# Three matrix projections of a gated linear-attention layer: from three fp32r products each to one plain fp32 product

## The chip, the cores and the metric

The kernel runs on one core of one Trainium2 chip. The metric is the device time of one launch in microseconds (us). The kernel before takes 194.22 us in the median of 3 runs (193.96 to 195.49).

## The reference, cut to what matters

The input `x` is 4 batches of 512 tokens with 256 features. It is layer-normed, projected to q, k, v and a low-rank gate, run through a chunked linear attention with 16 heads of 16 features, gated and normed by head, projected out, and multiplied by a small FFN branch that is rounded to fp8.

```python
xn = _layernorm(x, axis=-1)
q = silu(einsum('bnd,de->bne', xn, Wq).reshape(b, n, H, hd))    # k, v alike with Wk, Wv
o, _ = lightning_attn(q, k, v, log_decay)
gate = einsum('bnk,kd->bnd', einsum('bnd,dk->bnk', xn, Wg1), Wg2)
o = group_rmsnorm_fused_gate(o, gate, norm_w, H)
s = einsum('bnd,de->bne', o, Wo)
g = silu(ffn(xn, input2, scale, scale1))                        # both operands rounded to fp8
out = x + s * g
```

## The kernel before, in words

The work is cut into 16 chunks of 128 tokens, four to a batch. Each engine runs a prologue and then 18 steps, `step(i, j)`; the steps are software-pipelined by hand, so that one step holds different stages of neighbouring chunks. The order on each engine is the order in which its `step` function calls its helpers, and semaphores join the engines. For chunk n (`num(i, j)`) the step of TensorE (PE) does: the score products of n (`scores`, L1082, four groups r = 0 to 3), the gate product (L1068), the state update (L1108), the output projection of chunk n-2 (`project_o`, L1177), the K/V projection of chunk n+1 (`project_kv`), the Q/gate projection of chunk n+1 (`project_qg`), transposes for chunks n+1 and n+2 (L1009, L1021, L1063 and others), the products of masked scores with v (`from_chunk`, L1121), the FFN product (L1046), the products with the state (L1140), the transpose of the normed output (L1169), and the addition of the parts by products with the identity (`add_chunk`, L1150, L1153, L1157). Each score group goes through VectorE (DVE), which multiplies it with the decay mask (`mask`, L717). `from_chunk` waits for all four.

Three projections are computed to about fp32 accuracy from three fp32r products. Each operand is split in a high part, the value rounded to fp32r, and a low part, the rest: hi*hi + hi*lo + lo*hi, for each of two halves of the 256 contracted features. So each projection is 6 matmul calls: L1029, L1031 and L1034 for K/V (512 columns) and Q/gate (272 columns), and L1177 for the output projection (256 columns).

- ScalarE (ACT) makes the high part of the transposed x out of PSUM (`high_xT`, L484) and of the transposed output (`high_oT`, L537). DVE makes the low parts (`low_xT`, L703, `low_oT`, L783), after ACT.
- The weights are split once in the prologue: ACT makes the high parts of Wk and Wv (L576), DVE those of Wq and Wg1 (L854) and the low parts (`low_w`, L805). Wo, scaled by the norm weights (L828), is split in the first step (L628, L832).
- In the DVE prologue `low_w` and `low_xT` stand ahead of the layer-norm statistics of chunk 1 (L663), and `low_g1` (L707), which needs the Q/gate projection of chunk 0, comes some instructions later.

All other matmuls, but the gate product in fp32r and the FFN in bf16, are already plain fp32: `scores`, `state_step`, `from_chunk`, `from_state`, `add_chunk`. `keep_warm` (L1184) issues plain fp32 matmuls of 128 columns with no use but to keep PE busy: 11, 3 and 3 calls in the prologue and 6 in the tail.

Of the kernel before, what the change touches and what calls it, by code (L numbers as in the profile page):

```python
# [13 lines left out]
P = 128  # L14
# [3 lines left out]
def layer_kernel(nc, x, log_decay, Wq, Wk, Wv, Wo, Wg1, Wg2, norm_w, W2, scale, scale1, out):  # L18
# [34 lines left out]
    with ExitStack() as ctx:  # L53
# [9 lines left out]
        w_hi = sb("w_hi", [P, KH, NW], F32R)  # L63
        w_lo = sb("w_lo", [P, KH, NW], F32R)
        wo_f32 = sb("wo_f32", [P, KH, D])
        wo_scaled = sb("wo_scaled", [P, KH, D])
        wo_hi = sb("wo_hi", [P, KH, D], F32R)
        wo_lo = sb("wo_lo", [P, KH, D], F32R)
# [52 lines left out]
        xT_hi = sb("xT_hi", [P, KH, P], F32R)  # L121
        xT_lo = sb("xT_lo", [P, KH, P], F32R)
# [25 lines left out]
        oT_hi = sb("oT_hi", [P, KH, P], F32R)  # L148
        oT_lo = sb("oT_lo", [P, KH, P], F32R)
# [39 lines left out]
        s_whi = sem("w_hi_ready")  # L189
        s_wlo = sem("w_lo_ready")  # L190
# [20 lines left out]
        s_xThi = sem("xT_hi_ready")  # L211
        s_xTlo = sem("xT_lo_ready")
# [32 lines left out]
        s_oThi = sem("oT_hi_ready")  # L245
        s_oTlo = sem("oT_lo_ready")
# [230 lines left out]
        def _(act):  # L477
            a = nc.scalar

            def high_xT(i, j):  # L480
                act.wait_ge(s_xTps, num(i, j) + 1)

                need(act, s_qgps, num(i, j))
                a.activation(xT_hi[:], ps_xT, ACT.Copy).then_inc(s_xThi, 1)  # L484
# [88 lines left out]
            def high_w(a0, b0):  # L573

                for kk in range(KH):
                    a.activation(w_hi[:, kk, a0:b0], w_f32[:, kk, a0:b0], ACT.Copy).then_inc(s_whi, 1)  # L576

            def prologue(act):

                act.wait_ge(s_pool, 1)  # L580
                a.activation(table_load[:], eps_col[:], ACT.Exp)
                act.wait_ge(s_w, 32)
                high_w(0, Q0)
                normalise(0, 0)
                act.wait_ge(s_dvec, 3)
                a.activation(lag_decay[:], lag_logdecay[:], ACT.Exp).then_inc(s_actc, 1)
                high_xT(0, 0)
# [12 lines left out]
                copy_kT(0, 0)  # L600
                copy_qT(0, 0)
                copy_g1T(0, 0)
                high_xT(0, 1)
                act.wait_ge(s_pool, 15)
                part_v(0, 0)
                scale_y(0, 1)

            def step(act, i, j):
# [16 lines left out]
                if first:  # L625

                    act.wait_ge(s_woready, 2)
                    a.activation(wo_hi[:], wo_scaled[:], ACT.Copy).then_inc(s_woready, 1)  # L628
                if nxt:
                    copy_xqT(i, j + 1)  # L630
                if norm:
                    high_xT(i, j + 2)
# [9 lines left out]
                if known(i, j - 1):  # L642
                    high_oT(i, j - 1)
# [9 lines left out]
        def _(dve):  # L653
# [147 lines left out]

            def low_w(a0, b0, first):
                for kk in range(KH):
                    dve.wait_ge(s_whi, first + kk + 1)
                    v.tensor_tensor(w_lo[:, kk, a0:b0], w_f32[:, kk, a0:b0], w_hi[:, kk, a0:b0].bitcast(F32), ALU.subtract).then_inc(s_wlo, 1)  # L805
# [24 lines left out]
            def low_wo():  # L830
                dve.wait_ge(s_woready, 3)
                v.tensor_tensor(wo_lo[:], wo_scaled[:], wo_hi[:].bitcast(F32), ALU.subtract).then_inc(s_woready, 1)  # L832

            def prologue(dve):
# [54 lines left out]
                low_xT(0, 1)  # L889
# [3 lines left out]
            def step(dve, i, j):  # L893
# [8 lines left out]
                if not cur:  # L902
# [7 lines left out]
                    if back:  # L910
                        newton(8, RS_STEPS)
                        head_norm_last(i, j - 1)
                        low_oT(i, j - 1)
                    else:
                        add_x_last(i, j - 2)
                    return
                if not nxt:
# [11 lines left out]
                    low_oT(i, j - 1)  # L929
# [48 lines left out]
                if norm:  # L978
                    low_xT(i, j + 2)
                if first:  # L980
                    low_wo()
# [11 lines left out]
                if back:  # L993
                    low_oT(i, j - 1)
# [5 lines left out]
        def _(pe):  # L1000
# [23 lines left out]
            def project(i, j, dst, a, b, s_done, s_free, free):  # L1024

                pe.wait_ge(s_xThi, num(i, j) + 1)
                need(pe, s_free, free)
                for kk in range(KH):
                    t.matmul(dst, xT_hi[:, kk], w_hi[:, kk, a:b], start=(kk == 0), stop=False)  # L1029
                for kk in range(KH):  # L1030
                    t.matmul(dst, xT_hi[:, kk], w_lo[:, kk, a:b], start=False, stop=False)  # L1031
                pe.wait_ge(s_xTlo, num(i, j) + 1)
                for kk in range(KH):
                    mm = t.matmul(dst, xT_lo[:, kk], w_hi[:, kk, a:b], start=False, stop=(kk == KH - 1))  # L1034
# [137 lines left out]
            def project_o(i, j):  # L1172
                pe.wait_ge(s_oTlo, num(i, j) + 1)
                parts = [(oT_hi, wo_hi), (oT_hi, wo_lo), (oT_lo, wo_hi)]
                for n, (lhs, rhs) in enumerate(parts):
                    for kk in range(KH):
                        mm = t.matmul(ps_out, lhs[:, kk], rhs[:, kk], start=(n == 0 and kk == 0), stop=(n == 2 and kk == KH - 1))  # L1177
                mm.then_inc(s_outps, 1)
# [7 lines left out]
            def prologue(pe):  # L1186
# [4 lines left out]
                pe.wait_ge(s_wlo, 2)  # L1191
                project_kv(0, 0)
                pe.wait_ge(s_wlo, 4)
# [8 lines left out]
            def step(pe, i, j):  # L1202
# [86 lines left out]
```

## Time and profile before

| | us |
|---|---|
| median of 3 runs | 194.22 (193.96 to 195.49) |
| span of the profiled execution | 191.7 |
| PE busy | 171.6 |
| DVE busy | 158.9 |
| POOL (GpSimd) busy | 106.3 |
| ACT busy | 103.2 |

The profile lays out one execution. Busy times are sums over an engine's instructions. The chain of waits follows the work that ended last back from the end, at each step to what released it. L12 is line 12 of the kernel. The end of a matmul in the trace is modelled and overlaps the next one's start; the distance from start to start shows what a matmul costs in a row of them.

### The profile page before, as it was taken

How to read it: one execution, taken by the hardware profiler on the slowest of the kernel's cores; microseconds unless marked ns; L12 is line 12 of the kernel's file. 1: busy time of each engine (PE TensorE's matmuls, PEld its weight loads, DVE VectorE, ACT ScalarE, POOL GpSimd, SP SyncE). 2: the span in 40 equal slices, each digit the busy share in tenths (PEclk: the TensorE clock that was granted, in tenths of full speed). 3: DMA queues.
4: the chain of work that ended last, by engine and by line, in shares of the span. 5: the costliest groups of instructions: out<-in, count | busy, mean ns of one | idle time of the engine just before them, and what ended most of it. 6: DMA issues, size and time to landing. Idle time of an engine off the chain costs nothing.

```text
span 191.7 us, 6387 instructions
## 1 busy us (share of the span) xinstructions
PE 171.6 (90%) x1998; PEld 129.5 (68%) x1998; DVE 158.9 (83%) x548; ACT 103.2 (54%) x283; POOL 106.3 (55%) x181
## 2 busy tenths in 40 slices
PE   4867459999999999999999999999999999998392
PEld 4755238667776777777767777777767777776181
DVE  1869995889989898989897979898979798968672
ACT  3385336293848475665656473838383838372200
POOL 6954772555656465657574756565646556551210
PEclk9979966999999999999999999999999999999967
DMA  5383300000000010000000000000000000000000
GB/s 151 88 269 113 109 2 3 3 3 0 31 2 29 1 32 0 32 1 13 14 0 27 0 27 0 27 0 27 0 27 0 27 0 27 3 29 3 27 27 27
DMA packets 7199, 5.79 MB, mean 30 GB/s; under 512 B 1744, under 2 KB 7184, under 8 KB 7184
## 3 DMA queue, kind: packets, MB, share of 16 engines
q1 hardware_dynamic: 7184, 5.60, 9.3%
q8 instruction: 8, 0.13, 0.3%
q14 instruction: 7, 0.06, 0.1%
HBM read 3.50 MB, written 2.10 MB: 29 GB/s over the span
## 4 chain that ended last, share of the span: by engine, by line
PE 56%; DVE 20%; issue 12%; POOL 3%; DMA 3%; ACT 2%; DVEq 1%; SPq 1%; POOLq 0%; ACTq 0%
PE b_score L1082 9%; PE b_score L1121 9%; PE b_xo L1177 5%; PE b_att L1108 4%; DVE probs L717 4%; PE b_att L1140 3%; PE b_gate L1046 3%; PE b_xo L1169 3%; PE b_kv L1034 2%; PE b_kv L1031 2%; PE b_kv L1029 2%; PE b_qg L1029 2%; DVE shift L681 2%; PE b_att L1157 2%; DMA ld_row<-in_L_attn_log_decay_dram 2%
## 5 line engine op out<-in xcount | busy, mean ns | idle before, releaser
L717 DVE TENSOR_TENSOR probs<-b_score,decay_mask 128x512 f32<-128x512 f32 x64 | 43.5, 682 | 0.9 <-PE b_score L1082 0.5
L1082 PE MATMUL b_score<-qT,kT 32*64 32x128 f32 x512 | 31.6, 283 | 1.6 <-DVE probs L717 1.4
L545 ACT ACTIVATE xn<-x_sb,shift,rstd 128x256 f32 (+1 forms) x15 | 9.0, 602 | 42.3 <-DVE shift L681 42.3
L1082 PEld LDWEIGHTS b_score<-qT,kT 32*64 32x64 f32 x512 | 20.1, 132 | 12.3 <-issue 7.6
L374 POOL TENSOR_TENSOR state_c<-state,own_head 128x256 f32<-128x256 f32 x28 | 20.5, 734 | 11.6 <-DVE state L734 10.5
L344 POOL TENSOR_TENSOR e_sum<-e_y,e_magic 128x256 f32<-128x256 f32 x16 | 11.6, 727 | 20.5 <-DVE e_magic L692 20.5
L1121 PE MATMUL b_score<-probs,v_parity 128*32 128x128 f32 x512 | 17.9, 283 | 1.4 <-DVE probs L717 1.2
L383 POOL TENSOR_TENSOR on<-og,og_rs 128x256 f32<-128x256 f32 x15 | 9.3, 621 | 17.2 <-DVE og_rs L777 15.4
L1121 PEld LDWEIGHTS b_score<-probs,v_parity 128*32 128x32 f32 x512 | 13.6, 113 | 4.9 <-DVE probs L717 4.5
L775 DVE SCALAR_TENSOR_TENSOR og_half<-og_y,og_var 128x16 f32<-128x16 f32 x48 | 14.8, 309 | 0.7
L391 POOL TENSOR_TENSOR y<-sg,x_sb 128x256 f32<-128x256 f32 x15 | 10.9, 730 | 5.9 <-DVE sg L788 5.9
L688 DVE TENSOR_SCALAR e_exp<-e_y 128x256 int32<-128x256 int32 x16 | 4.7, 293 | 10.6 <-ACT e_y L561 10.6
L526 ACT ACTIVATE qT<-b_qk,head_parity 128x256 f32<-128x256 f32 x32 | 13.3, 472 | 0.0
L1108 PE MATMUL b_att<-kv,kd 64*64 64x64 f32 x224 | 12.8, 234 | 0.0
L347 POOL TENSOR_TENSOR e_q<-e_sum,e_magic 128x256 bf16<-128x256 f32 x16 | 12.0, 752 | 1.3
L335 POOL TENSOR_TENSOR var_eps<-mean_var,eps_col 128x1 f32<-128x1 f32 x16 | 3.2, 201 | 17.0 <-DVE mean_var L673 17.0
L681 DVE SCALAR_TENSOR_TENSOR shift<-mean_var,rstd 128x1 f32<-128x1 f32 x16 | 10.9, 683 | 1.8 <-POOL rstd L337 0.8
L353 POOL TENSOR_TENSOR xq<-e_q,e_nan 128x256 bf16<-128x256 bf16 x16 | 10.7, 670 | 2.5 <-DVE e_nan L698 2.5
L1029 PE MATMUL b_kv<-w_hi,xT_hi 128*128 128x512 f32 x32 | 10.3, 401 | 1.8 <-ACT xT_hi L484 1.8
L1108 PEld LDWEIGHTS b_att<-kv,kd 64*64 64x64 f32 x224 | 8.9, 136 | 4.3 <-issue 2.2
L1184 PE MATMUL b_score<-ident 128*128 128x128 f32 x46 | 9.4, 384 | 2.5 <-POOL ident L402 2.5
L537 ACT ACTIVATE oT_hi<-b_xo 128x256 fp32r<-128x256 f32 x16 | 6.1, 384 | 9.4 <-PE b_xo L1169 8.4
(136 smaller groups left out, 470.9 us busy)
## 6 DMA issues: line engine op xcount, KB each, us to landing
out_dram<-y SPq DMA_DIRECT2D x16, 128.0 KB, 1.7
x_sb<-in_L_attn_x_dram SPq DMA_DIRECT2D x3, 512.0 KB, 3.4
x_sb<-in_L_attn_x_dram SPq DMA_DIRECT2D x1, 384.0 KB, 4.6
w_f<-in_L_attn_Wk_dram SPq DMA_DIRECT2D x1, 256.0 KB, 2.8
w_f<-in_L_attn_Wv_dram SPq DMA_DIRECT2D x1, 256.0 KB, 3.0
w_f<-in_L_attn_Wq_dram SPq DMA_DIRECT2D x1, 256.0 KB, 3.0
w_f<-in_L_ffn_input_dram SPq DMA_DIRECT2D x1, 256.0 KB, 4.0
wo_f<-in_L_attn_Wo_dram SPq DMA_DIRECT2D x1, 256.0 KB, 3.8
```

Of the source, the lines that this page charges most:

```text
L344: g.tensor_tensor(e4_sum[:], e4_y[:], e4_magic[:], ALU.add).then_inc(s_e4p, 1)
L347: g.tensor_tensor(e4_q[:], e4_sum[:], e4_magic[:], ALU.subtract).then_inc(s_e4p, 1)
L374: g.tensor_tensor(dst[:].rearrange("p k (b c) -> p k b c", b=2), state[:].unsqueeze(2).broadcast_to([P, KH, 2, C]), own_head[:].rearrange( ...
L391: g.tensor_tensor(y[:, j % 2, :], sg[:], xs, ALU.add).then_inc(s_y, 1)
L526: a.activation(qT[:, u, :, par, :], ps_qT, ACT.Copy, scale=head_parity[:, par:par + 1]).then_inc(s_qkT, 1)
L681: v.scalar_tensor_tensor(out=shift[:, u], in0=mean_var[:, u, 0:1], scalar=-1.0, in1=rstd[:, u], op0=ALU.mult, op1=ALU.mult).then_inc(s_shi ...
L717: v.tensor_tensor(probs[:, r].rearrange("p i (b c) -> p i b c", b=2), b_score[r % 2][:, 0:4 * C].rearrange("p (i c) -> p i c", i=4).unsque ...
L775: ins = v.scalar_tensor_tensor(out=og_half[:], in0=og_y2[:], scalar=-0.5, in1=og_var[:], op0=ALU.mult, op1=ALU.mult)
L1029: t.matmul(dst, xT_hi[:, kk], w_hi[:, kk, a:b], start=(kk == 0), stop=False)
L1082: mm = t.matmul(b_score[r % 2][c * C:c * C + C, half * 2 * C:(half + 1) * 2 * C], kT[rows, u, half, c * C:c * C + C], qT[rows, u, half, :, ...
L1108: mm = t.matmul(ps_state[b * C:b * C + C, half, :], kd[rows, u, cols], kv[rows, u, D + cols.start:D + cols.stop], start=True, stop=True)
L1121: mm = t.matmul(ps_avT[32 * r:32 * r + 32, half, :], v_parity[:, u, par * D + half * P + 32 * r:par * D + half * P + 32 * r + 32], probs[: ...
```

## The change

The K/V, Q/gate and output projections use the fp32 operands as they are, with two matmul calls each in place of six. The splits of weights and activations are gone, with their tiles and semaphores. ACT's copies of the transposed x and output out of PSUM stay and now write fp32. The gate product of low rank stays in fp32r with its split.

```diff
-            def high_xT(i, j):
+            def copy_xT(i, j):
                 act.wait_ge(s_xTps, num(i, j) + 1)
                 need(act, s_qgps, num(i, j))
-                a.activation(xT_hi[:], ps_xT, ACT.Copy).then_inc(s_xThi, 1)
+                a.activation(xT[:], ps_xT, ACT.Copy).then_inc(s_xT, 1)
...
-            def high_oT(i, j):
+            def copy_oT(i, j):
                 act.wait_ge(s_oTps, num(i, j) + 1)
                 need(act, s_outps, num(i, j))
-                a.activation(oT_hi[:], ps_oT, ACT.Copy).then_inc(s_oThi, 1)
+                a.activation(oT[:], ps_oT, ACT.Copy).then_inc(s_oT, 1)
...
-                act.wait_ge(s_w, 32)
-                high_w(0, Q0)
                 normalise(0, 0)
...
-                    act.wait_ge(s_woready, 2)
-                    a.activation(wo_hi[:], wo_scaled[:], ACT.Copy).then_inc(s_woready, 1)
...
-            def low_xT(i, j):
-                dve.wait_ge(s_xThi, num(i, j) + 1)
-                need(dve, s_qgps, num(i, j))
-                v.tensor_tensor(xT_lo[:], ps_xT, xT_hi[:].bitcast(F32), ALU.subtract).then_inc(s_xTlo, 1)
...
-            def low_oT(i, j):
-                dve.wait_ge(s_oThi, num(i, j) + 1)
-                need(dve, s_outps, num(i, j))
-                v.tensor_tensor(oT_lo[:], ps_oT, oT_hi[:].bitcast(F32), ALU.subtract).then_inc(s_oTlo, 1)
...
-                low_w(0, Q0, 0)
-                low_xT(0, 0)
-                dve.wait_ge(s_wq, 32)
-                for kk in range(KH):
-                    v.tensor_copy(w_hi[:, kk, Q0:NW], w_f32[:, kk, Q0:NW]).then_inc(s_whi, 1)
-                low_w(Q0, NW, 2)
                 stats(0, 1)
...
-                low_xT(0, 1)
                 quantise_w2()
...
-                if norm:
-                    low_xT(i, j + 2)
-                if first:
-                    low_wo()
...
-                if back:
-                    low_oT(i, j - 1)
...
             def project(i, j, dst, a, b, s_done, s_free, free):
-                pe.wait_ge(s_xThi, num(i, j) + 1)
+                pe.wait_ge(s_xT, num(i, j) + 1)
                 need(pe, s_free, free)
                 for kk in range(KH):
-                    t.matmul(dst, xT_hi[:, kk], w_hi[:, kk, a:b], start=(kk == 0), stop=False)
-                for kk in range(KH):
-                    t.matmul(dst, xT_hi[:, kk], w_lo[:, kk, a:b], start=False, stop=False)
-                pe.wait_ge(s_xTlo, num(i, j) + 1)
-                for kk in range(KH):
-                    mm = t.matmul(dst, xT_lo[:, kk], w_hi[:, kk, a:b], start=False, stop=(kk == KH - 1))
+                    mm = t.matmul(dst, xT[:, kk], w_f32[:, kk, a:b], start=(kk == 0), stop=(kk == KH - 1))
                 mm.then_inc(s_done, 1)
...
                 if known(i, j + 3):
-                    pe.wait_ge(s_xTlo, num(i, j) + 4)
+                    pe.wait_ge(s_xT, num(i, j) + 4)
...
             def project_o(i, j):
-                pe.wait_ge(s_oTlo, num(i, j) + 1)
-                parts = [(oT_hi, wo_hi), (oT_hi, wo_lo), (oT_lo, wo_hi)]
-                for n, (lhs, rhs) in enumerate(parts):
-                    for kk in range(KH):
-                        mm = t.matmul(ps_out, lhs[:, kk], rhs[:, kk], start=(n == 0 and kk == 0), stop=(n == 2 and kk == KH - 1))
+                pe.wait_ge(s_oT, num(i, j) + 1)
+                for kk in range(KH):
+                    mm = t.matmul(ps_out, oT[:, kk], wo_scaled[:, kk], start=(kk == 0), stop=(kk == KH - 1))
                 mm.then_inc(s_outps, 1)
...
-                pe.wait_ge(s_wlo, 2)
+                pe.wait_ge(s_w, 32)
                 project_kv(0, 0)
-                pe.wait_ge(s_wlo, 4)
+                pe.wait_ge(s_wq, 32)
                 project_qg(0, 0)
...
-                        pe.wait_ge(s_woready, 4)
+                        pe.wait_ge(s_woready, 2)
```

## Rows read from the trace of the kernel before

**Rows 1.** The page: busy time by engine, and the chain's shares by engine.

```profile
PE 171.6 (90%) x1998; PEld 129.5 (68%) x1998; DVE 158.9 (83%) x548; ACT 103.2 (54%) x283; POOL 106.3 (55%) x181
...
PE 56%; DVE 20%; issue 12%; POOL 3%; DMA 3%; ACT 2%; DVEq 1%; SPq 1%; POOLq 0%; ACTq 0%
```

**Rows 2.** Busy time by stretch; stretches run from one `from_chunk` (L1121) to a later one.

```profile
core 0: us, PE busy (x) PEld busy (x) DVE busy (x) ACT busy (x) POOL busy (x), PEclk, DMA share, GB/s
31.00:41.05 10.05, 9.64 (x117) 7.03 (x117) 7.72 (x27) 5.83 (x17) 4.17 (x7) 0.93 0.01 3
...
60.73:70.63 9.90, 9.90 (x128) 7.51 (x132) 8.61 (x33) 5.91 (x17) 5.46 (x9) 1.00 0.05 15
...
90.56:100.40 9.84, 9.53 (x116) 7.14 (x116) 8.83 (x34) 6.21 (x18) 6.14 (x10) 1.00 0.04 13
...
41.05:169.58 128.53, 127.51 (x1590) 95.52 (x1594) 114.18 (x420) 77.68 (x219) 77.05 (x125) 1.00 0.04 14
```

**Rows 3.** The chain of waits, 95 to 118 us: start, length, engine and line.

```profile
99.67 0.69 DVE probs L717
...
100.40 1.08 PE b_score L1121 x32
...
102.77 0.45 PE b_att L1157 x4
...
104.63 0.90 PE b_xo L1177 x6
105.53 0.45 PE b_kv L1029 x2
...
107.48 0.45 PE b_qg L1029 x2
107.93 0.25 PE b_qg L1031 x2
```

**Rows 4.** Timeline of PE, 100 to 111.3 us: start, length with drain, instruction.

```profile
105.13 0.40 PE L1177 MATMUL b_xo<-wo_hi,oT_lo 128*128 128x256 f32 x2
105.36 0.61 PE L1029 MATMUL b_kv<-w_hi,xT_hi 128*128 128x512 f32 x2
...
109.32 0.29 PE L1021 MATMUL b_gate<-ident_bf,xq 128*128 128x128 bf16 x2
109.45 0.39 PE L1009 MATMUL b_xo<-ident,xn 128*128 128x128 f32 x2
109.67 0.38 PE L1061 MATMUL b_qk<-ident,q 128*128 128x128 f32 x2
```

**Rows 5.** Groups by line and shape, DVE: busy, mean ns, idle before.

```profile
L783 DVE TENSOR_TENSOR oT_lo<-b_xo,oT_hi 128x256 fp32r<-128x256 f32 x16 | 6.7, 418 | 1.3 <-ACT oT_hi L537 1.3
L703 DVE TENSOR_TENSOR xT_lo<-b_xo,xT_hi 128x256 fp32r<-128x256 f32 x16 | 6.7, 417 | 1.7 <-ACT xT_hi L484 1.7
```

**Rows 6.** Timeline of DVE, 0 to 35 us.

```profile
10.97 0.42 DVE L703 TENSOR_TENSOR xT_lo<-b_xo,xT_hi 128x256 fp32r<-128x256 f32 x1 [1.08 <-ACT xT_hi L484]
...
12.87 0.41 DVE L663 BATCH_NORM_STATS2 bn<-x_sb 128x6 f32<-128x256 f32 x1
...
15.62 0.18 DVE L707 TENSOR_TENSOR g_stack<-b_qg,g_stack 128x32 fp32r<-128x32 f32 x1
...
28.05 1.46 DVE L717 TENSOR_TENSOR probs<-b_score,decay_mask 128x512 f32<-128x512 f32 x2
```

**Rows 7.** Busy time by stretch, start-up (columns as in rows 2).

```profile
28.00:30.00 2.00, 2.00 (x21) 1.55 (x18) 1.91 (x6) 1.30 (x4) 1.30 (x3) 0.50 0.03 8
```

**Rows 8.** Timeline of PE, 159 to 192 us: the tail.

```profile
183.49 2.66 PE L1184 MATMUL b_score<-ident 128*128 128x128 f32 x12
```

**Rows 9.** The chain of waits in the last step.

```profile
187.18 0.43 DVE oT_lo L783
...
187.66 0.99 PE b_xo L1177 x6
```

More of the change, by code:

```diff
@@ L62, in layer_kernel @@
         w_f32 = sb("w_f32", [P, KH, NW])
-        w_hi = sb("w_hi", [P, KH, NW], F32R)
-        w_lo = sb("w_lo", [P, KH, NW], F32R)
         wo_f32 = sb("wo_f32", [P, KH, D])
         wo_scaled = sb("wo_scaled", [P, KH, D])
-        wo_hi = sb("wo_hi", [P, KH, D], F32R)
-        wo_lo = sb("wo_lo", [P, KH, D], F32R)
         nw_col = sb("nw_col", [P, KH])
@@ L120, in layer_kernel @@
         xq = sb("xq", [P, 2, D], BF16)
-        xT_hi = sb("xT_hi", [P, KH, P], F32R)
-        xT_lo = sb("xT_lo", [P, KH, P], F32R)
+        xT = sb("xT", [P, KH, P])
         xqT = sb("xqT", [P, KH, P], BF16)
@@ L147, in layer_kernel @@
         on = sb("on", [P, D])
-        oT_hi = sb("oT_hi", [P, KH, P], F32R)
-        oT_lo = sb("oT_lo", [P, KH, P], F32R)
+        oT = sb("oT", [P, KH, P])
         sg = sb("sg", [P, D])
@@ L210, in layer_kernel @@
         s_xqTps = sem("xqT_in_psum")
-        s_xThi = sem("xT_hi_ready")
-        s_xTlo = sem("xT_lo_ready")
+        s_xT = sem("xT_ready")
         s_xqT = sem("xqT_ready")
@@ L244, in layer_kernel @@
         s_oTps = sem("oT_in_psum")
-        s_oThi = sem("oT_hi_ready")
-        s_oTlo = sem("oT_lo_ready")
+        s_oT = sem("oT_ready")
         s_outps = sem("out_in_psum")
@@ L571, in copy_avT @@
                 a.activation(avT[:], ps_avT, ACT.Copy).then_inc(s_av, 1)
-            def high_w(a0, b0):
-                for kk in range(KH):
-                    a.activation(w_hi[:, kk, a0:b0], w_f32[:, kk, a0:b0], ACT.Copy).then_inc(s_whi, 1)
             def prologue(act):
@@ L586, in prologue @@
                 a.activation(lag_decay[:], lag_logdecay[:], ACT.Exp).then_inc(s_actc, 1)
-                high_xT(0, 0)
+                copy_xT(0, 0)
                 act.wait_ge(s_small, 64)
@@ L602, in prologue @@
                 copy_g1T(0, 0)
-                high_xT(0, 1)
+                copy_xT(0, 1)
                 act.wait_ge(s_pool, 15)
@@ L631, in step @@
                 if norm:
-                    high_xT(i, j + 2)
+                    copy_xT(i, j + 2)
                 if nxt:
@@ L642, in step @@
                 if known(i, j - 1):
-                    high_oT(i, j - 1)
+                    copy_oT(i, j - 1)
                 if nxt:
@@ L800, in add_x_last @@
                 v.tensor_tensor(y[:, j % 2, :], sg[:], x_sb[:, num(i, j), :], ALU.add).then_inc(s_y, 1)
-            def low_w(a0, b0, first):
-                for kk in range(KH):
-                    dve.wait_ge(s_whi, first + kk + 1)
-                    v.tensor_tensor(w_lo[:, kk, a0:b0], w_f32[:, kk, a0:b0], w_hi[:, kk, a0:b0].bitcast(F32), ALU.subtract).then_inc(s_wlo, 1)
             def quantise_w2():
@@ L828, in scale_wo @@
                     v.tensor_scalar(wo_scaled[:, kk], wo_f32[:, kk], nw_col[:, kk:kk + 1], None, ALU.mult).then_inc(s_woready, 1)
-            def low_wo():
-                dve.wait_ge(s_woready, 3)
-                v.tensor_tensor(wo_lo[:], wo_scaled[:], wo_hi[:].bitcast(F32), ALU.subtract).then_inc(s_woready, 1)
             def prologue(dve):
@@ L928, in step @@
                     gate_o(i, j)
-                    low_oT(i, j - 1)
                     return
@@ L977, in step @@
                 newton(10, RS_STEPS)
-                if norm:
-                    low_xT(i, j + 2)
-                if first:
-                    low_wo()
                 if nxt:
@@ L992, in step @@
                     gate_o(i, j)
-                if back:
-                    low_oT(i, j - 1)
             steps(step, prologue)(dve)
@@ L1172, in project_o @@
             def project_o(i, j):
-                pe.wait_ge(s_oTlo, num(i, j) + 1)
-                parts = [(oT_hi, wo_hi), (oT_hi, wo_lo), (oT_lo, wo_hi)]
-                for n, (lhs, rhs) in enumerate(parts):
-                    for kk in range(KH):
-                        mm = t.matmul(ps_out, lhs[:, kk], rhs[:, kk], start=(n == 0 and kk == 0), stop=(n == 2 and kk == KH - 1))
+                pe.wait_ge(s_oT, num(i, j) + 1)
+                for kk in range(KH):
+                    mm = t.matmul(ps_out, oT[:, kk], wo_scaled[:, kk], start=(kk == 0), stop=(kk == KH - 1))
                 mm.then_inc(s_outps, 1)
```

3 lines of the change are left out of this document (removed).

## The prediction

> **What bounds the kernel now.** I read the page first. PE is busy for 90% of the span and DVE for 83%, so either could set the pace; in the chain PE has 56% and DVE 20% [rows 1]. To see which one ends last inside a step I took busy time by stretch, with cuts at the start of each `from_chunk`. There are 13 such intervals from 41.05 to 169.58 us, one for each of chunks 2 to 14, and each holds one projection of each kind. Over those 128.53 us PE is idle for 128.53 - 127.51 = 1.02 us at full clock [rows 2]. Most intervals look like the one from 60.73: PE busy 9.90 of 9.90. One in four looks like that from 90.56: PE busy 9.53 of 9.84, and there the chain runs through DVE to the last `mask` (L717) and on into `from_chunk` [rows 2, 3]. Three of these with some 0.31 us each make up most of the 1.02. So the kernel is bound by PE, with DVE close behind. That matters: work taken from DVE buys little, work added to PE is paid in full.
>
> **What one fp32r product costs.** In a row of them the distance between starts counts, not the length, which holds the drain. Two fp32r matmuls of 256 columns take 105.36 - 105.13 = 0.23 us, so 0.115 each [rows 4]. In the chain, pairs of 512 columns take 0.45 to 0.47 (0.228 each), pairs of 272 columns 0.25 (0.125 each). The first pair after other work takes longer: Q/gate's 0.45 in place of 0.25, and the output projection's six take 0.90, 0.21 more than 6 x 0.115 [rows 3]. I call these 0.20 and 0.21 the entry.
>
> **What one plain fp32 product costs.** No row has a plain fp32 matmul of over 128 columns, so this is the disputed price. `add_chunk` (L1157) makes two calls, and the chain shows x4: every plain fp32 call becomes two matmul instructions, a fp32r call only one (six calls, x6) [rows 3]. Those four take 0.45 us, 0.1125 for each pass of 128 columns [rows 3], nearly what a fp32r matmul needs for 256. So a pass streams at half the columns per time, and there are two: a plain product costs about four times a single-rate one of its size. A second row supports the half rate: two bf16 transposes of 128 columns take 109.45 - 109.32 = 0.13, two fp32 ones 109.67 - 109.45 = 0.22 [rows 4]. A third has full fp32 matmuls back to back at a lowered clock: 12 of 128 columns in 2.66 us [rows 8]. Three fp32r products against one that costs four: PE pays more, not less, although a third of the instructions goes.
>
> With passes that scale by columns from 0.1125:
> - K/V, 512 columns: before 6 x 0.228 = 1.37; after 4 x 0.45 = 1.80; +0.43.
> - Q/gate, 272 columns: before 0.95 with the entry; after 4 x 0.239 + 0.20 = 1.16; +0.21.
> - Output, 256 columns: before 0.90; after 4 x 0.225 + 0.21 = 1.11; +0.21.
>
> Sum +0.85 us per interval. Bounds: if a pass costs just its columns at 2.4 GHz and half rate (0.427, 0.227, 0.213) it is +0.34, +0.16, +0.16, so +0.66. If it costs twice the fp32r matmul of its size (0.456, 0.250, 0.230) it is +0.45, +0.25, +0.23, so +0.93. I take +0.85: the row of a real plain pass carries it. The entry stays in both, since the full-array load that it exposes is needed for either type.
>
> The Trainium skill ("FP8 and Floating Point Precision", TensorE Precision Notes) counts true fp32 as four passes through the array. By that, four of the measured fp32r times per product, K/V would take 8 x 0.228 = 1.82, Q/gate 8 x 0.125 + 0.20 = 1.20, output 8 x 0.115 + 0.21 = 1.13, which is the upper bound and not the value from the 128-column row. The skill ("TensorE: Matmul & The Clock Gate", Weight-path perf modes) also says that fast weight load is on for 128 weights whose type is not fp32; by that, this change would lose it. The trace doesn't bear out a loss at this size: four plain passes with their loads keep 0.1125 from start to start, and the passes here are two to four times as long, so a slower load stays covered.
>
> **13 intervals.** 13 x 0.85 = +11.1 us.
>
> **What DVE gets back.** `low_xT` and `low_oT` cost 0.417 and 0.418 us once per chunk [rows 5]. Both leave DVE in every interval, and `low_oT` stands ahead of the next masks, in the loop that ties with PE. With 0.8 us less on DVE and 0.85 more on PE, the three DVE-ended intervals become PE-ended, and PE's idle time is absorbed: -1.0. If it weren't, the cost is 1.0 more. ACT's two copies per chunk stay, at the same size; fp32 in place of fp32r as output I price at nothing, since the fp32 copies of that size on ACT stand beside them in the same steps; ACT is busy for 54% [rows 1].
>
> **The interval from 31.00 to 41.05** has K/V and Q/gate but no output projection, and PE is idle for 0.41 of it [rows 2]. +0.64 on PE, and the idle time goes, since DVE loses `low_xT`: +0.2.
>
> **The start, up to 31.00.** DVE loses much: `low_w`, the cast of Wq, `low_xT`. The statistics of chunk 1, at 12.87, come 1.7 us or so after `xT_lo` ended up ahead of them at 10.97 [rows 6] and can come earlier. But `low_g1` at 15.62 [rows 6] waits for the Q/gate projection of chunk 0, through ACT, and the two projections of chunk 0 get longer by 0.64, by about twice that where the clock is at half. DVE is held there until about 16, loses a few tenths, and gains 0.42 back from the `low_xT` of chunk 1. What is late next is the FFN weight work and then PE. Net 0, within 0.5 either way. `low_wo` and `wo_hi` in the first step lie beside PE's work and give nothing.
>
> **The tail, from 169.58.** The output projection of chunk 13 stands before a score group: +0.2. For the last chunk `oT_lo` goes, 0.43 with its hop of 0.04, and the six matmuls of 0.99 grow by 0.21 [rows 9]: -0.3. Net -0.1.
>
> **Sum.** 11.1 - 1.0 + 0.2 + 0.0 - 0.1 = +10.2 us, span 191.7 + 10.2 = 201.9. The median lies 194.22 - 191.7 = 2.5 above the span, which the change doesn't touch: 204.4 us.
>
> **The likeliest case's own range.** With +0.66 per interval 13 x 0.66 = 8.6, so 201.9; with +0.93 it is 12.1, so 205.4; idle time not absorbed adds 1.0, and the start moves it by 0.5 either way: 201.4 to 206.9.
>
> **The rivals.**
> - *The start's clock turns out otherwise.* From about 26 to 32 us PE works at the lower level, 1.2 GHz, after it was idle between pieces of work; the stretch 28 to 30 shows 0.50 [rows 7]. The longer projections just before fill part of that idle time. If the clock then stayed at 2.4 GHz, the PE work from 27.1 to 32 would be some 2.4 shorter. But `from_chunk` waits for masks, which DVE ends at 28.05 + 1.46 = 29.5 [rows 6] where PE starts at 31.00, so 1.5 is won: 202.9. For it: the projections fill time. Against: the wait for the FFN weights on DVE stays. 10%, most of it in the range.
> - *The weight loads of plain fp32 show.* If each of the 12 passes exposed its load, as the entry does with half of 0.2, that is 1.2 per interval: 13 x 1.2 = 15.6 more, 220. Against: the loads hide behind passes of 128 columns [rows 3]. 4%.
> - *DVE, not PE, is the real bound.* Then PE's added time would hide in its idle time and the 0.83 from DVE would come off. PE's idle time is only 1.02 of 128.53 [rows 2], so at most one or two tenths of the added 11.1 could hide; for a result within 1% the extra would have to be below 0.15 to 0.2 per interval. 2%.
> - *Faster: wide passes stream at full rate.* If a plain pass of 256 columns or more ran at the rate of fp32r, four passes would replace six: -2 x (0.228 + 0.125 + 0.115) = -0.94 per interval on PE, with -0.83 on DVE, so about -0.85: 194.2 - 11 = 183. It decides below a pass cost of 1.5 fp32r matmuls of the same size, where four passes equal six. For it: nothing wide and plain is in the trace. Against: a half rate in three places at 128 columns, transposes included [rows 3, 4, 8]. 5%.
>
> **How the numbers follow.** Forecast 79%, start's clock 10%, exposed loads 4%, DVE-bound 2%, faster 5%. The range 201.4 to 206.9 of the first two leaves out the other three (11%) and some error in the scaling; I keep 201.3 to 207.0. A change of about 1%, 1.9 us, is what a measurement of this kernel can tell from none. Faster 5%, same 2%, slower 93%.
>
> **What would show it.** Right: the lines of K/V, Q/gate and output show 4 instructions per projection; K/V takes about 1.80 from first start to the next work; intervals between `from_chunk` starts are 10.6 to 10.8, with PE's idle time near 0 in all 13; DVE idles 1.5 us or more in each. Wrong: pairs of wide passes at 0.45 or below (the full rate), gaps in the weight loads' row of 0.1 before each pass, or intervals near 9.9 with DVE ahead of PE in the chain. The whole sum hangs on one number, the time of a wide plain pass, taken from a narrow one.

## The result and the profile after

The changed kernel is slower: 202.23 us in the median of 5 runs (200.72 to 202.91) against 194.12 (193.96 to 195.49). The ratio is 1.0385, 95% interval 1.0333 to 1.0438. All ratios here leave out executions that took over 1.5% more than the fastest of the same kernel. In the profiled executions the span goes from 191.7 to 198.8, +7.1.

The line numbers have moved: L974 is now the K/V and the Q/gate projection, L1115 the output projection, L1061 `from_chunk`, L1022 `scores`, L1097 `add_chunk`, L691 `mask`.

First the page after. Against [rows 1] PE is busy for 10.3 us more, DVE for 10.1 less, and the chain has moved from a mixture to PE.

```profile
PE 181.9 (92%) x1902; PEld 121.8 (61%) x1902; DVE 148.8 (75%) x509; ACT 102.5 (52%) x280; POOL 106.0 (53%) x181
...
PE 80%; DVE 10%; issue 3%; DMA 2%; ACT 2%; POOL 2%; SPq 1%; DVEq 0%; ACTq 0%; POOLq 0%
```

Busy time by stretch of the changed kernel: all 13 intervals together, and two of them (columns as in [rows 2]).

```profile
41.15:176.80 135.65, 135.65 (x1513) 89.85 (x1516) 108.78 (x393) 78.76 (x220) 76.87 (x125) 1.00 0.04 13
93.44:103.53 10.09, 10.09 (x114) 6.69 (x118) 8.07 (x30) 6.12 (x18) 6.13 (x10) 1.00 0.00 1
103.53:114.00 10.47, 10.47 (x122) 7.00 (x126) 8.58 (x31) 6.12 (x18) 5.44 (x9) 1.00 0.07 25
```

PE has no idle time left: 135.65 of 135.65, where [rows 2] had 127.51 of 128.53. DVE idles 135.65 - 108.78 = 26.9 us, 2.1 per interval.

The chain of waits of the changed kernel through one interval shows what the projections cost.

```profile
103.53 1.01 PE b_score L1061 x32
104.54 0.32 PE b_gate L986 x2
...
105.83 0.45 PE b_att L1097 x4
...
107.69 1.06 PE b_xo L1115 x4
108.75 1.72 PE b_kv L974 x4
110.46 0.58 PE b_score L1022 x8
111.05 1.11 PE b_qg L974 x4
112.16 0.58 PE b_score L1022 x8
...
114.00 1.01 PE b_score L1061 x32
```

Each projection is four instructions, as forecast. K/V takes 1.72 us where it was three pairs of 0.45 to 0.47, 1.38, Q/gate 1.11 where they had 0.95, the output projection 1.06 where it was 0.90 [rows 3]: +0.34, +0.16, +0.16, together +0.66 per interval, not +0.85.

By part, with the cuts at the starts of `from_chunk` as the timelines show them (the chain puts them some hundredths later):

| stretch | before | after | change | forecast |
|---|---|---|---|---|
| start to the first `from_chunk` | 30.93 | 31.09 | +0.16 | 0.0 |
| first to second | 10.12 | 9.99 | -0.13 | +0.2 |
| the 13 intervals | 128.46 | 135.65 | +7.19 | +10.1 |
| from the 15th to the end | 22.19 | 22.07 | -0.12 | -0.1 |
| span | 191.7 | 198.8 | +7.1 | +10.2 |

The medians differ by more than the spans, 8.1. The traced execution of the changed kernel was the fastest of its five, 200.72, and the time around the first `from_chunk` differs from one execution to the next. From the first to the second `from_chunk` the trace of price_list (below), which runs the same steps as the kernel before, has 10.53 at a granted clock of 0.89 in place of 10.12 at 0.93; that of plain_with_low, whose 13 intervals are those of the changed kernel, has 11.10 at 0.84 in place of 9.99 at 0.95. So one trace of each kernel can't tell whether the +0.2 of that row is right. The 13 intervals themselves repeat within 0.1 us in every trace of the kernel before's steps.

The intervals come in four kinds by the chunk's place in its batch. Typical lengths in us; the interval of chunk 14, the last, is shorter than its kind and has a column of its own:

| chunk n modulo 4 | 2 | 3 | 0 | 1 | n = 14 | sum of 13 |
|---|---|---|---|---|---|---|
| before | 9.83 to 9.92 | 9.84 | 9.80 to 9.83 | 10.08 | 9.57 | 128.46 |
| after | 10.47 | 10.10 | 10.47 | 10.76 | 10.25 | 135.65 |
| plain_with_low | 10.47 | 10.10 | 10.47 | 10.75 | 10.26 | 135.65 |
| six_no_low | 9.84 | 9.79 | 9.82 | 10.07 | 9.58 | 128.19 |
| only_out_plain | 9.99 | 9.78 | 9.98 | 10.26 | 9.78 | 129.84 |
| out_split_again | 10.32 | 9.95 | 10.32 | 10.61 | 10.11 | 133.70 |
| one_product_filled | 9.84 | 9.78 | 9.61 | 10.07 | 9.17 | 127.07 |

### The profile page after: what moved, and what is told of

Its sections match the earlier page's. It is cut to its first block, busy times and chain, and to the rows that moved or that the text cites. A ratio compares the mean times of both kernels' runs of the same rounds, so it can differ in the third digit from the quotient of the medians.

```text
span 198.8 us, 6123 instructions
## 1 busy us (share of the span) xinstructions
PE 181.9 (92%) x1902; PEld 121.8 (61%) x1902; DVE 148.8 (75%) x509; ACT 102.5 (52%) x280; POOL 106.0 (53%) x181
## 4 chain that ended last, share of the span: by engine, by line
PE 80%; DVE 10%; issue 3%; DMA 2%; ACT 2%; POOL 2%; SPq 1%; DVEq 0%; ACTq 0%; POOLq 0%
PE b_kv L974 14%; PE b_score L1022 13%; PE b_qg L974 9%; PE b_xo L1115 8%; PE b_score L1061 8%; PE b_att L1048 5%; PE b_att L1080 4%; PE b_xo L1109 3%; PE b_gate L986 3%; PE b_att L1097 2%; PE b_gate L1008 2%; PE b_qk L1001 2%; PE b_qk L1003 2%; DMA ld_row<-in_L_attn_log_decay_dram 2%; PE b_gate L966 2%
## 5 line engine op out<-in xcount | busy, mean ns | idle before, releaser
L691 DVE TENSOR_TENSOR probs<-b_score,decay_mask 128x512 f32<-128x512 f32 x64 | 43.8, 687 | 6.7 <-PE b_score L1022 5.7
L974 PE MATMUL b_kv<-w_f,xT 128*128 128x512 f32 x64 | 31.6, 617 | 1.9 <-ACT xT L474 1.9
L1022 PEld LDWEIGHTS b_score<-qT,kT 32*64 32x64 f32 x512 | 20.1, 132 | 20.6 <-issue 13.0
L1022 PE MATMUL b_score<-qT,kT 32*64 32x128 f32 x512 | 31.6, 282 | 0.9 <-DVE probs L691 0.6
L1115 PE MATMUL b_xo<-wo_scaled,oT 128*128 128x256 f32 x64 | 19.0, 422 | 0.9 <-ACT oT L527 0.9
L974 PE MATMUL b_qg<-w_f,xT 128*128 128x272 f32 x64 | 19.7, 433 | 0.0
L974 PEld LDWEIGHTS b_kv<-w_f,xT 128*128 128x128 f32 x64 | 12.1, 193 | 10.8 <-issue 10.0
L1061 PE MATMUL b_score<-probs,v_parity 128*32 128x128 f32 x512 | 17.8, 281 | 0.5 <-DVE probs L691 0.5
L715 DVE TENSOR_TENSOR qdT<-b_qk,q_decay 128x256 f32<-128x256 f32 x16 | 6.8, 423 | 12.2 <-ACT qT L516 12.2
L1061 PEld LDWEIGHTS b_score<-probs,v_parity 128*32 128x32 f32 x512 | 13.4, 112 | 3.5 <-issue 1.8
L974 PEld LDWEIGHTS b_qg<-w_f,xT 128*128 128x128 f32 x64 | 11.5, 198 | 4.9 <-issue 3.4
L1115 PEld LDWEIGHTS b_xo<-wo_scaled,oT 128*128 128x128 f32 x64 | 11.3, 197 | 3.3 <-ACT oT L527 1.4
```

The lines of the kernel that those rows point to most:

```text
L691: v.tensor_tensor(probs[:, r].rearrange("p i (b c) -> p i b c", b=2), b_score[r % 2][:, 0:4 * C].rearrange("p (i c) -> p i c", i=4).unsque ...
L974: mm = t.matmul(dst, xT[:, kk], w_f32[:, kk, a:b], start=(kk == 0), stop=(kk == KH - 1))
L1022: mm = t.matmul(b_score[r % 2][c * C:c * C + C, half * 2 * C:(half + 1) * 2 * C], kT[rows, u, half, c * C:c * C + C], qT[rows, u, half, :, ...
L1061: mm = t.matmul(ps_avT[32 * r:32 * r + 32, half, :], v_parity[:, u, par * D + half * P + 32 * r:par * D + half * P + 32 * r + 32], probs[: ...
L1115: mm = t.matmul(ps_out, oT[:, kk], wo_scaled[:, kk], start=(kk == 0), stop=(kk == KH - 1))
```

## Experiments

**Where the 3 us less than forecast come from.** Two theories: A, a wide plain pass is cheaper than forecast; B, DVE's relief gave back more than PE's idle time. Four kernels cross the two: PE's products and DVE's subtractions, separately.

**six_no_low** keeps the six fp32r products and takes the two subtractions per chunk off DVE; PE multiplies with the low parts of chunk 0 throughout, so the output is less accurate.

```diff
             def low_xT(i, j):
+                if not (isinstance(i, int) and num(i, j) == 0):
+                    return
...
             def low_oT(i, j):
+                if not (isinstance(i, int) and num(i, j) == 0):
+                    return
...
-                pe.wait_ge(s_xTlo, num(i, j) + 1)
+                pe.wait_ge(s_xTlo, 1)
...
-                pe.wait_ge(s_oTlo, num(i, j) + 1)
+                pe.wait_ge(s_oTlo, 1)
+                pe.wait_ge(s_oThi, num(i, j) + 1)
```

> The kernel before with its six fp32r products, but VectorE makes the low parts of x and of the output once, for chunk 0, and every later chunk multiplies with those stale parts; so only VectorE's two subtractions of 0.42 us each per chunk are left out and TensorE does the same products. Theory A (a wide plain pass is simply cheaper than forecast, +0.66 per interval in place of +0.85, and VectorE's relief is worth little more than TensorE's idle time of 1.02 us): 1.0 to 1.6 us faster than before, intervals that end in DVE gone. Theory B (VectorE's relief is what made the result cheaper than forecast, worth 3 us or more): 3 us or more faster.

Measured: ratio 1.0022 (0.9983 to 1.006), no difference; the 13 intervals 128.19 against 128.46. Both theories miss, B by far. DVE's 0.84 us per interval are worth 0.27 us in all 13. Its busy time fell from 114.18 [rows 2] to 106.75, yet PE's idle time only went from 1.02 to 0.84:

```profile
41.55:169.74 128.19, 127.35 (x1587) 95.43 (x1587) 106.75 (x395) 77.47 (x219) 77.08 (x125) 1.00 0.04 14
```

The chain in the interval that had ended on DVE shows why. Where `oT_lo` had stood, DVE now waits for ACT (start, length, engine, line, of six_no_low):

```profile
93.88 0.42 DVE og L750
94.30 0.02 issue
94.33 0.43 ACT og_sq L566
...
95.09 0.42 DVE bn L663
95.50 0.08 DVE og_sum L756
...
99.98 0.69 DVE probs L719
100.67 0.04 issue
100.71 1.08 PE b_score L1125 x32
```

`gate_o` makes og, ACT squares it, and `sum_heads`, which DVE has to pass in order before its second mask, needs the squares. So this is not DVE short of time: it is a loop of waits through DVE, ACT and PE, from one `from_chunk` to the next.

**plain_with_low** is the changed kernel with both subtractions back, into tiles that nobody reads, and PE waiting for them.

```diff
+            def low_xT(i, j):
+                dve.wait_ge(s_xT, num(i, j) + 1)
+                need(dve, s_qgps, num(i, j))
+                v.tensor_tensor(x_rest[:], ps_xT, xT[:], ALU.subtract).then_inc(s_xr, 1)
...
                 for kk in range(KH):
+                    if kk == KH - 1:
+                        pe.wait_ge(s_xr, num(i, j) + 1)
                     mm = t.matmul(dst, xT[:, kk], w_f32[:, kk, a:b], start=(kk == 0), stop=(kk == KH - 1))
...
-                pe.wait_ge(s_oT, num(i, j) + 1)
+                pe.wait_ge(s_or, num(i, j) + 1)
```

> The changed kernel with both subtractions of VectorE put back for every chunk (their results are not used), and TensorE waiting for them where the kernel before does. Theory A: TensorE's interval is 0.3 to 0.66 us longer than before, which covers VectorE's 0.84, so it takes what the changed kernel takes, within 0.5 us: some 1.038 times before. Theory B: VectorE ends the intervals again, 3 us slower than the changed kernel, 1.053 times before.

Measured: 1.0378 (1.0324 to 1.0432), the changed kernel's own ratio. The 13 intervals take 135.65, the same to a hundredth, with DVE busy for 6.5 us more. Theory B falls.

```profile
41.87:177.52 135.65, 135.65 (x1508) 89.82 (x1509) 115.27 (x420) 78.89 (x220) 77.05 (x125) 1.00 0.04 13
```

**only_out_plain** and **out_split_again** move one projection each way.

```diff
-                parts = [(oT_hi, wo_hi), (oT_hi, wo_lo), (oT_lo, wo_hi)]
-                for n, (lhs, rhs) in enumerate(parts):
-                    for kk in range(KH):
-                        mm = t.matmul(ps_out, lhs[:, kk], rhs[:, kk], start=(n == 0 and kk == 0), stop=(n == 2 and kk == KH - 1))
+                for kk in range(KH):
+                    mm = t.matmul(ps_out, oT[:, kk], wo_scaled[:, kk], start=(kk == 0), stop=(kk == KH - 1))
```

This is the core of the first, made in the kernel before, with `low_oT` empty; the second makes it backwards in the changed kernel, with `low_oT` and Wo's split back.

> The kernel before with the output projection alone in plain fp32, K/V and Q/gate still in three fp32r products. Theory A: 13 intervals at +0.16, two more output projections, minus about 1.0 of TensorE's idle time that goes since low_oT leaves VectorE: +1.0 to +1.5 us, ratio 1.005 to 1.008. The forecast's price of +0.21 would give +1.7 to +2.2, ratio 1.009 to 1.011. Theory B: faster than before by 1 us or more, since half of VectorE's relief is there and little of TensorE's cost.

> The changed kernel with the output projection split into three fp32r products again (six matmuls, low_oT back on VectorE, Wo split in the first step). Theory A: 15 or so output projections at -0.16 on TensorE, VectorE's 0.42 hidden: 2.1 to 2.5 us faster than the changed kernel, ratio to before 1.025 to 1.028. Theory B: VectorE's work comes back and takes the gain away: as slow as the changed kernel or slower, 1.038 and more.

Measured: only_out_plain 1.0038 (1.0015 to 1.0062), 13 intervals 129.84, so +1.38. Theory A's range for the ratio, 1.005 to 1.008, was a little high, though the measured interval reaches it, and the medians of all executions, 195.25 and 194.25, give 1.005. out_split_again 1.0228 (1.0177 to 1.0278), below theory A's 1.025 to 1.028, but again its interval reaches them; 13 intervals 133.70, so -1.95 from the changed kernel, which is 0.15 in each of the four kinds. In only_out_plain three kinds grow by 0.07 to 0.19, and the kind n = 3 modulo 4 shrinks by 0.06. The same edit is worth 0.15 where PE sets the pace and nothing where the loop of waits does.

**price_list**: the disputed price by itself. The kernel before, with eight calls in a row of each kind at the end of PE's program (one execution).

```diff
             steps(step, prologue)(pe)
+            acc = b_score[1]
+            for n in (64, 128, 256, 512):
+                for _ in range(8):
+                    t.matmul(acc[:, 0:n], ident[:], w_f32[:, 0, 0:n], start=True, stop=True)
+            for n in (64, 128, 256, 512):
+                for _ in range(8):
+                    t.matmul(acc[:, 0:n], xT_hi[:, 0], w_hi[:, 0, 0:n], start=True, stop=True)
+            for n in (64, 128, 256):
+                for _ in range(8):
+                    t.matmul(acc[:, 0:n], xqT[:, 0], w2_fp8[:, 0, 0:n], start=True, stop=True)
```

> The kernel before with groups of 8 products in a row added at the end of TensorE's program, of no use to the output: plain fp32 of 64, 128, 256 and 512 columns, then fp32r and bf16. It is slower by their time. From start to start, theory A: a plain fp32 call shows two passes of 0.110, 0.217 and 0.430 us at 128, 256 and 512 columns, its columns at half of 2.4 GHz plus a fixed few ns; fp32r 0.115 at 256 and 0.228 at 512, which is more than its columns at 2.4 GHz (0.107, 0.213). The forecast's scaling would show 0.225 and 0.450 for plain passes of 256 and 512. At 64 columns the load of the 128 weight columns, seen as 0.11 at the entry of a group, should be the floor for both types.

Timeline of PE in price_list: start, length of the group with one drain, line, shape, count.

```profile
189.03 1.61 PE L1266 MATMUL b_score<-w_f,ident 128*128 128x64 f32 x13
...
190.76 1.61 PE L1266 MATMUL b_score<-w_f,ident 128*128 128x128 f32 x13
...
192.65 3.40 PE L1266 MATMUL b_score<-w_f,ident 128*128 128x256 f32 x15
...
195.89 6.60 PE L1266 MATMUL b_score<-w_f,ident 128*128 128x512 f32 x15
...
203.71 0.94 PE L1269 MATMUL b_score<-w_hi,xT_hi 128*128 128x128 f32 x7
...
205.49 2.02 PE L1269 MATMUL b_score<-w_hi,xT_hi 128*128 128x512 f32 x8
...
207.59 0.50 PE L1272 MATMUL b_score<-w_fp,xqT 128*128 128x128 bf16 x6
```

From start to start, in us, at full clock, from the starts of the single instructions:

| columns | plain fp32, each of two passes | fp32r | bf16 |
|---|---|---|---|
| 64 | 0.112 | 0.112 | 0.029 |
| 128 | 0.112 | 0.112 | 0.056 |
| 256 | 0.216 | 0.119 | 0.109 |
| 512 | 0.429 | 0.232 | |

A pass of 64 columns takes as long as one of 128: 1.61 us for 13 in both rows. So 0.112 is not the streaming of 128 columns, it is a floor. fp32r stands on the same floor, bf16 does not. The load of the 128 columns of weights is the likely cause: it is the same in all these rows but for the type, and no run loads fewer columns of weights to show it. Above it a plain pass takes its columns at half of 2.4 GHz and some 2.5 ns: 512/1.2 = 426.7 against 429. Theory A holds; the forecast's 0.450 and 0.225 are too high.

**The gaps in the start.** The forecast had a rival about the clock between 26 and 32 us. In the changed kernel it stood at 0.50 there, as in [rows 7]. **before_filled** and **after_filled** put products of no use into PE's gaps of the first step.

```diff
+            def fill(count):
+                for _ in range(count):
+                    t.matmul(ps_out[:, 0:P], ident[:], ident[:], start=True, stop=True)
...
                 if nxt:
                     project_kv(i, j + 1)
+                if first:
+                    fill(5)
                 if cur:
                     scores(i, j, 2)
                 if first:
+                    fill(6)
                     transpose_xq(0, 0)
                 if nxt:
                     project_qg(i, j + 1)
                 if first:
+                    fill(6)
```

In after_filled the counts are 2, 6 and 3.

> The kernel before with 5, 6 and 6 plain fp32 products of 128 columns, of no use to the output, set into the three gaps of TensorE between 20 and 27 us (beside unused PSUM columns). If the clock stays at 2.4 GHz through 26 to 32 us, TensorE's work from 27.1 to 31 us gets shorter until VectorE's masks end at 29.5: 1.0 to 1.5 us faster, ratio 0.992 to 0.995, and the first from_chunk starts at 29.6 to 30. If the clock falls anyway, nothing changes or it is 0.2 slower.

> The changed kernel with 2, 6 and 3 such products in the same gaps, which are shorter there. As in the kernel before with the gaps filled: 1.0 to 1.5 us faster than the changed kernel, 1.031 to 1.033 times before, if the clock holds; 1.038 if not.

Measured: before_filled 0.9893 (0.9854 to 0.9931), after_filled 1.0244 (1.0191 to 1.0296). The first gains 1.1% of the kernel before, and its interval just reaches the expected 0.992; the second gains 1.4% against the changed kernel's 1.0385, more than expected. The medians of before_filled and of the kernel before beside it, 192.3 and 193.91, are 1.6 us apart. Of before_filled, busy time by stretch:

```profile
26.00:28.00 2.00, 1.73 (x18) 1.22 (x17) 1.97 (x5) 0.48 (x3) 1.18 (x3) 1.00 0.02 4
28.00:30.00 2.00, 1.96 (x42) 1.60 (x41) 2.00 (x7) 2.00 (x7) 1.52 (x4) 1.00 0.00 0
```

The clock is 1.00 where it was 0.50 [rows 7], and the first `from_chunk` starts at 29.42 instead of 30.93. PE's work ahead of it and DVE's last mask end within 0.02 us of each other there, at 29.39 and 29.37. The interval after it drops from 10.12 to 9.47, which I had not priced. The 13 intervals stay at 128.50.

**before_filled_tail** adds the same in the tail, where before_filled's trace had the clock at 0.50 from 179 us on and the stretch to the end took 23.2 in place of 22.2.

```diff
                     add_chunk(i, j)
+                    keep_warm(8)
                 if back and not cur:
-                    keep_warm(6)
+                    keep_warm(10)
```

> The kernel before with the three gaps of the start filled as in before_filled, and in the tail eight products of no use after the last add_chunk and ten in place of six ahead of the last transpose. In before_filled the clock was at 0.50 from 179 us on and the tail took 23.2 us against 22.2 before. With the tail filled: 22.0 to 22.4, so 0.5 to 1.0 us faster than before_filled, ratio 0.985 to 0.987. If the tail's clock doesn't depend on it: 0.989.

Measured: 0.9874 (0.9824 to 0.9924), 191.81 us in the median, against 192.3 of before_filled. The traced tail takes 22.24, as expected, at full clock up to 187.6 us:

```profile
182.00:184.00 2.00, 1.40 (x13) 1.21 (x11) 1.86 (x7) 0.00 (x0) 0.72 (x1) 1.00 0.00 0
```

The two ratios' intervals overlap, and the kernel before has 22.19 in its trace without any filling of the tail. So it is not shown that this filling helps: one trace of each has the tail 1.0 us shorter, and no more than that is known. before_filled and before_filled_tail are faster than either kernel of the case.

**How far is PE the bound?** **one_product** leaves out two of the three products, and DVE's subtractions after chunk 0, so the output is less accurate.

```diff
-                for kk in range(KH):
-                    t.matmul(dst, xT_hi[:, kk], w_hi[:, kk, a:b], start=(kk == 0), stop=False)
-                for kk in range(KH):
-                    t.matmul(dst, xT_hi[:, kk], w_lo[:, kk, a:b], start=False, stop=False)
-                pe.wait_ge(s_xTlo, 1)
-                for kk in range(KH):
-                    mm = t.matmul(dst, xT_lo[:, kk], w_hi[:, kk, a:b], start=False, stop=(kk == KH - 1))
+                for kk in range(KH):
+                    mm = t.matmul(dst, xT_hi[:, kk], w_hi[:, kk, a:b], start=(kk == 0), stop=(kk == KH - 1))
...
-                parts = [(oT_hi, wo_hi), (oT_hi, wo_lo), (oT_lo, wo_hi)]
+                parts = [(oT_hi, wo_hi)]
```

> The kernel before with only the hi*hi product of each projection (lower precision) and VectorE's low parts of activations left out after chunk 0. TensorE loses 4 x (0.228 + 0.125 + 0.115) = 1.87 us per interval, VectorE 0.84. If TensorE alone set the pace, 13 x 1.87 = 24 us would be won. I expect VectorE to take over as the bound after about 1 us: it was busy for 8.8 us per interval, 7.95 without the low parts, plus its waits, so intervals of 8.6 to 9.1 and 180 to 185 us, ratio 0.93 to 0.95.

Measured: 1.1072 (1.1017 to 1.1127), **slower by over 20 us**, with less work on PE and on DVE. The expectation was wrong in sign. Timeline of PE and busy time by stretch, one_product:

```profile
95.06 0.52 PE L1033 MATMUL b_qg<-w_hi,xT_hi 128*128 128x272 f32 x2
97.21 1.12 PE L1081 MATMUL b_score<-qT,kT 32*64 32x128 f32 x8 [1.63 <-DVE state L736]
```

```profile
96.00:98.00 2.00, 0.79 (x8) 0.72 (x8) 1.92 (x8) 1.25 (x4) 1.43 (x3) 0.79 0.00 0
98.00:100.00 2.00, 2.00 (x19) 1.63 (x16) 1.97 (x9) 1.14 (x5) 1.15 (x2) 0.50 0.19 65
100.00:102.00 2.00, 2.00 (x35) 1.54 (x33) 0.36 (x2) 1.23 (x4) 1.31 (x2) 0.50 0.00 1
```

PE gets ahead and waits 1.63 us for DVE's state, one of ten such waits of up to 1.7 us; then the clock is at 0.50, 1.2 GHz, and everything behind it takes twice as long: `from_chunk`, 1.08 us before, takes 1.94 here. The mean clock over the run was 0.775, against 0.958.

**one_product_filled** tells whether it is the clock: five products of no use per step ahead of that wait.

```diff
                 if cur:
+                    if nxt:
+                        pe.wait_ge(s_qd, num(i, j) + 1)
+                        fill(5)
                     state_waits(i, j, 1)
```

> The kernel with only the hi*hi products (lower precision, stale low parts not used), and in each step five plain fp32 products of 128 columns, of no use to the output, ahead of TensorE's wait for the state (1.1 us of the 1.87 us per interval that the left-out products took). Theory C (the version with one product is slow because TensorE, idle for 1.6 us in its steps, gets the 1.2 GHz clock for the next pieces): with the gap filled the clock is 1.00 through the steady part, intervals 9.1 to 9.5 us, ratio 0.95 to 0.98. Rival (VectorE's chain of waits sets intervals of 11 us by itself): unchanged at 1.10.

Measured: 0.9875 (0.9829 to 0.992). The clock is 1.00 in the whole steady part and 22 us come back, so theory C holds for the slow run. But the intervals are not 9.1 to 9.5: they are 9.84, 9.78, 9.61 and 10.07, some 0.2 or less from the kernel before (the last, 9.17, is 0.4 from it), though PE has 1.87 - 1.12 = 0.75 us and DVE 0.84 us less in each. PE is idle for 0.4 to 0.8 us of each (columns as in [rows 2]):

```profile
72.49:82.56 10.07, 9.46 (x122) 6.85 (x122) 8.36 (x33) 6.10 (x18) 6.14 (x10) 1.00 0.05 16
82.56:92.39 9.83, 9.18 (x122) 6.86 (x122) 8.35 (x33) 6.13 (x18) 6.14 (x10) 1.00 0.04 13
```

So the kernel before has a second bound right under PE's: a loop of waits. The chain of waits of one_product_filled shows it in the interval from 82.56:

```profile
82.56 1.08 PE b_score L1120 x32
83.64 0.34 PE b_gate L1045 x2
...
84.38 0.51 ACT e_y L561
84.89 0.02 issue
84.91 0.30 DVE e_exp L688
...
85.52 0.42 DVE og L750
85.94 0.02 issue
85.97 0.43 ACT og_sq L566
...
91.66 0.69 DVE probs L719
```

Of its 9.83 us PE holds 1.42, `from_chunk` and the FFN product, and the added products are not in it.

**two_products** leaves out lo*hi alone, again with DVE's subtractions after chunk 0.

```diff
-                pe.wait_ge(s_xTlo, 1)
-                for kk in range(KH):
-                    mm = t.matmul(dst, xT_lo[:, kk], w_hi[:, kk, a:b], start=False, stop=(kk == KH - 1))
...
-                parts = [(oT_hi, wo_hi), (oT_hi, wo_lo), (oT_lo, wo_hi)]
+                parts = [(oT_hi, wo_hi), (oT_hi, wo_lo)]
```

> The kernel before without the lo*hi product of the three projections (lower precision) and without VectorE's low parts of activations. TensorE loses 2 x (0.228 + 0.125 + 0.115) = 0.94 us per interval. If TensorE's pace alone counts: intervals of 8.9 to 9.0, 12 us faster, ratio 0.94. If VectorE's chain ends the intervals once TensorE has gaps, as in one interval of four before: 9.2 to 9.6 us, ratio 0.96 to 0.98. If the gaps bring the clock down: slower than before. I expect the middle one, with the clock at risk.

Measured: 1.0004 (0.9962 to 1.0046), no difference; its runs scatter from 192.7 to 199.7, and the traced one took 197.0. In its trace the intervals with full clock are 9.79, 9.60 and 10.07, the loop's lengths again and without any product of no use in the steps, and five are longer, 10.20 to 11.02; three stretches of 9 or 10 us among them show a granted clock of 0.83 to 0.85 in place of 1.00, though PE never waited for longer than 0.7 us in this part. Two stretches of it:

```profile
80.00:90.00 10.00, 9.79 (x115) 7.14 (x115) 7.25 (x28) 6.08 (x17) 5.35 (x9) 0.83 0.05 16
100.00:110.00 10.00, 9.18 (x113) 6.51 (x113) 8.20 (x30) 5.95 (x17) 5.66 (x10) 1.00 0.04 13
```

Both of the feared things happened and none of the expected gain came.

## Why the prediction was right, and where it was not

The direction, the range (201.3 to 207.0) and the mechanism held: PE pays for four passes in place of six. The point, 204.4, was 2.2 above the median. The change was forecast at +10.2; the spans show +7.1 and the medians +8.1. That the median comes nearer than the spans is luck: the extra 1.0 lies outside the 13 intervals, as far as plain_with_low's trace shows it in a slower start, and no term of the sum stands for it. Of the signs named for being right, the four instructions, PE's idle time near 0 and DVE's 1.5 us or more came true, but K/V took 1.72 and not 1.80, and only one kind of interval, 10.76, lies in 10.6 to 10.8; the others are 10.10 and 10.47.

- **Two instructions per plain product**: right, four per projection in the trace after.
- **The price of a wide plain pass**: this is the term that was mis-sized. It took 0.1125 per 128 columns from `add_chunk` and scaled it by columns. price_list shows that figure to be a floor which 64 columns meet too. The lower bound of the same part, columns at half rate and 2.4 GHz, +0.66, is what the three projections cost, to a hundredth. It is worth 13 x 0.19 = 2.5 of the 3 us. Between the two bounds I chose "by the row of a real plain pass", when that row was the narrowest of all, where the load of the weights isn't covered by the pass.
- **The entry stays in both**: right, Q/gate has 1.11 - 4 x 0.229 = 0.19 of it after (0.229 is 272/1.2 and the 2.5 ns), the output projection 1.06 - 4 x 0.216 = 0.20.
- **PE's idle time is absorbed**: right in outcome (0.00 idle in 135.65), larger in size (13 x 0.66 - 7.19 = 1.4 in place of 1.0), and wrong in its reason. In size, most of the missing 0.4 seems to be `from_chunk`: where it had to wait it takes 1.08 in the chain instead of 1.01, and its 13 lengths add up to 13.60 before and 13.15 after. The forecast gave it to DVE's relief. plain_with_low puts all that work back and nothing changes; six_no_low takes it away and nothing changes. PE's own growth covers the wait.
- **"The kernel is bound by PE, with DVE close behind"**: half right. Near PE's own time lies a loop of waits. With PE's own time taken as that of after less 0.66, that is 9.81, 9.44, 9.81 and 10.10 by kind, and the loop's lengths from one_product_filled, 9.84, 9.78, 9.61 and 10.07, the larger of the two is within 0.06 of the interval before in all four kinds, but for the few at 9.92. The same sum gives 9.59 for chunk 14 (measured 9.57), and with the output projection's 0.16 added to PE's time 9.97, 9.78, 9.97 and 10.26 for only_out_plain, measured 9.99, 9.78, 9.98 and 10.26. The subtraction assumes that PE's pieces add up; no run shows PE's time in the kernel before by itself. What makes some intervals 9.92 stays open.
- **The rule on weight loads**: the forecast said that a loss of the Trainium skill's fast weight load ("TensorE: Matmul & The Clock Gate", Weight-path perf modes) would stay covered. It did. price_list goes beyond it: fp32r stands on the same floor of 0.112 as plain fp32, and only bf16 is below, so by these rows there was nothing to lose here. By the four passes of "FP8 and Floating Point Precision" (the Trainium skill, TensorE Precision Notes), taken at bf16's 0.109 for 256 columns, a plain product would take 0.436; measured 2 x 0.216 = 0.432. The rule agrees once it is applied to a streaming time without the floor.
- **The start**: right. `low_g1` runs at 16.14 us in the trace after ("about 16"), and the statistics of chunk 1 at 11.63 instead of 12.87 win nothing. +0.16.
- **The tail**: -0.12, forecast -0.1.
- **The rivals**: the faster case (wide passes at full rate) is out, 0.429 against 0.232. Exposed loads: no gap before the wide passes. The start's clock didn't change with the change itself, but it could be changed by hand, for 1.1% (1.6 us between the medians), which the forecast had priced at 1.5.

## What to carry to other kernels

A plain fp32 matmul costs two passes at half the columns per time. So in TensorE's time alone, three fp32r products are cheaper than one plain product at 256 columns (3 x 0.119 against 2 x 0.216) and at 512 (3 x 0.232 against 2 x 0.429), and dearer at 128 (3 x 0.112 against 2 x 0.112). Before a small instruction's time is scaled to a large one, look for a second size in the trace that shows what part of it is a floor. And when an engine is busy for 99% of a stretch, this still doesn't say that less work on it makes the stretch shorter: here a loop of waits lay within tenths of a microsecond, and the time taken from PE came back as idle time and a lower clock.

## What the runs showed of the hardware that I had not expected

- Less work on TensorE made the kernel 10.7% slower. After PE had waited 1.63 us within a step, the next pieces ran at 1.2 GHz, and 32 matmuls took 1.94 us in place of 1.08. Five products of no use per step turned that into 0.9875 times before. In two_products the clock fell for some stretches too, with no wait of PE over 0.7 us.
- With 128 columns of fp32 or fp32r weights a pass takes 0.112 us from start to start, for 64 columns of output as for 128; with bf16 it is 0.029 at 64.
- Between executions of one kernel the time varies, from 191.4 to 195.5 us in the runs of before, with the mean clock between 0.93 and 0.97. The traces of kernels that kept a full clock in the steady part place the low clock in the first 35 us and the tail. With three gaps filled by 17 useless products 6 runs lay between 191.95 and 192.64, but it is not shown that this narrows the scatter: with the tail filled too, one of 6 took 194.03.
